# Two residual convolution blocks on one core: the low gate of the second half moves from ScalarE to VectorE

## What is computed

```
def _L0_conv_ref(x, w1, ..., w2, ..., lambdas):
    xr = tile(x, (1, 4, 1, 1))
    out = conv3x3(sign(xr), sign(w1), groups=4)
    out = relu(batchnorm(out, bn1))
    out = conv3x3(sign(out), sign(w2), groups=4)
    out = batchnorm(out, bn2) * repeat(lambdas, 64)
    out = out.reshape(B, 4, 64, H, W).sum(axis=1)
    return relu(out + x)

def _L1_conv_ref(x, masks, conv_w, in_gamma, in_beta):
    m = resize(masks, 28 x 28)
    mid = x * m
    atten = sigmoid(conv7x7([mean_c(mid), max_c(mid), m]))
    out = mid * atten
    rn = instance_norm(out) * in_gamma + in_beta
    return relu(5 * rn)

x = x + _L0_conv_ref(group_norm(x), ...)
x = x + _L1_conv_ref(group_norm(x), ...)
```

## Time and profile before

| what | value |
|---|---|
| median of 3 runs | 228.22 us (227.88 to 228.31) |
| the profiled execution, whole | 227.68 us |
| its span from first to last instruction | 225.9 us |
| granted TensorE clock, mean | 0.980 of full speed |
| TensorE busy (PE) | 198.2 us, 88% |
| ScalarE busy (ACT) | 173.8 us, 77% |
| GpSimd busy (POOL) | 154.3 us, 68% |
| VectorE busy (DVE) | 152.0 us, 67% |

### The profile page before, as it was taken

The page is one execution under the profiler, slowest core; times in us unless marked ns, Lnnn a source line. Parts: engine busy times, 40 slices in busy tenths (PEclk is TensorE's granted clock), DMA queues, the critical chain, the costliest instruction groups (busy, mean ns, idle before and its releaser), DMA issues.

```text
span 225.9 us, 8997 instructions
## 1 busy us (share of the span) xinstructions
PE 198.2 (88%) x3807; PEld 123.7 (55%) x3807; DVE 152.0 (67%) x440; ACT 173.8 (77%) x230; POOL 154.3 (68%) x216
## 2 busy tenths in 40 slices
PE   8998997999899989889998998899999998698810
PEld 3456554465566566546564665466556655366710
DVE  2676365965846887677686854775657565988874
ACT  2785889888769878798899878989899888341392
POOL 8532273727142996799769978797879877947960
PEclk9999999999999999999999999999999999999965
DMA  6998004642217040744073404431453236124117
GB/s 199 334 299 303 15 4 112 198 141 68 81 61 231 3 145 7 228 131 145 3 207 86 147 1 151 141 97 52 121 173 73 75 97 193 64 84 144 74 71 284
DMA packets 12429, 28.48 MB, mean 126 GB/s; under 512 B 2293, under 2 KB 4213, under 8 KB 12389
## 3 DMA queue, kind: packets, MB, share of 16 engines
q1 hardware_dynamic: 11653, 26.84, 38.5%
q10 hardware_dynamic: 736, 1.06, 1.5%
HBM read 21.29 MB, written 6.61 MB: 124 GB/s over the span
## 4 chain that ended last, share of the span: by engine, by line
PE 41%; POOL 19%; ACT 12%; DVE 11%; issue 9%; DMA 4%; SPq 1%; ACTq 1%; POOLq 0%; DVEq 0%
PE c L1025 10%; PE c L1004 10%; PE small L1082 6%; POOL X L437 6%; PE small L1070 5%; POOL o L432 3%; ACT S L599 3%; DMA att_b<-attention_rows 3%; ACT acc L622 3%; DVE RD L799 2%; POOL o L419 2%; DVE bnst L740 2%; ACT word L584 2%; PE y L1045 2%; DMA o<-in_w 2%
## 5 line engine op out<-in xcount | busy, mean ns | idle before, releaser
L1025 PE MATMUL c<-S,w2t 64*32 64x392 f16 x2304 | 55.1, 331 | 7.9 <-DVE RD L799 7.3
L1004 PE MATMUL c<-E,w1t 64*128 64x420 f16 (+1 forms) x576 | 54.5, 330 | 0.9 <-ACT E L578 0.7
L799 DVE SCALAR_TENSOR_TENSOR RD<-RD,c 128x784 f16<-128x784 f16 x32 | 30.8, 964 | 29.5 <-ACT RD L606 29.4
L1025 PEld LDWEIGHTS c<-S,w2t 64*32 64x32 f16 x2304 | 31.8, 92 | 26.9 <-issue 14.0
L1004 PEld LDWEIGHTS c<-E,w1t 64*128 64x128 f16 x576 | 25.5, 94 | 25.2 <-issue 7.7
L740 DVE BATCH_NORM_STATS2 bnst<-X 128x6 f32<-128x392 f32 x64 | 32.6, 552 | 6.1 <-POOL X L437 3.3
L584 ACT ACTIVATE word<-c 128x840 int32<-128x840 f32 (+1 forms) x32 | 26.0, 812 | 9.3 <-PE c L1004 9.3
L419 POOL TENSOR_TENSOR o<-o,mask_b 128x784 f32<-128x784 f32 x14 | 26.1, 1868 | 9.2 <-ACT o L628 9.2
L594 ACT ACTIVATE S<-word,thr_high 128x840 f16<-128x840 int16 (+1 forms) x32 | 30.4, 951 | 0.6
L437 POOL TENSOR_TENSOR X<-X,acc 128x784 f32<-128x784 f32 x14 | 26.0, 1856 | 6.3 <-ACT acc L622 6.3
L599 ACT ACTIVATE S<-word,thr_low_act 128x840 f16<-128x840 uint16 (+1 forms) x32 | 30.0, 937 | 0.0
(11 more groups left out here) (135 smaller groups left out, 266.6 us busy)
## 6 DMA issues: line engine op xcount, KB each, us to landing
X<-in_x SPq DMA_DIRECT2D x16, 392.0 KB, 6.1
mask_b<-mask_rows SPq DMA_DIRECT2D x32, 196.0 KB, 3.5
out<-o SPq DMA_DIRECT2D x15, 392.0 KB, 3.9
att_b<-attention_rows SPq DMA_DIRECT2D x28, 196.0 KB, 4.6
o<-in_w ACTq DMA_DIRECT2D x1, 576.0 KB, 5.2
o<-in_masks SPq DMA_DIRECT2D x1, 512.0 KB, 8.9
band<-in_band SPq DMA_DIRECT2D x1, 441.0 KB, 10.1
cs<-in_cst SPq DMA_DIRECT2D x1, 434.0 KB, 6.2
```

The costliest lines, as they stand in the source:

```text
L799: dve.scalar_tensor_tensor(RD[:, hh, 1, :], RD[:, hh, 0, :], -IMG / TINY, second_sums(t, hh), ALU.mult, ALU.add).then_inc(low2, 1)
L1004: mm = pe.matmul(c1[:, 512 - n * (1 - i):512 + n * i], w1t[64 * i:64 * i + 64, s, :], window(START[i][hh], ROWS[hh], s, E[64 * i:64 * i + ...
L1025: mm = pe.matmul(second_bank(t, hh)[at:at + Q32, LOW + HALF * i:LOW + HALF * (i + 1)], w2t[64 * r:64 * r + 64, s, q, :], window(RH * half_ ...
```

## The change

The low gate of the second half (hh = 1) is made by VectorE, with a comparison instead of a steep sigmoid: 1 where the low 16 bits of the word are above `thr_low`, else 0. It has a semaphore of its own, `gated_low1`. ScalarE keeps the high gates of both halves and the low gate of the first.

```
--- before.py
+++ after.py
             def words1(t, hh):
                 if has(t):
                     act.wait_ge(conv1_done, 2 * t + hh + 1)
+                    if hh:
+                        wait(act, gated_low1, t)
                     act.activation(word1_of(hh), first_sums(hh), ACT.Copy, bias=WORD / 2,
                                    scale=WORD / IMG).then_inc(worded1, 1)
...
-            def low_gates(t, hh):
-                if has(t):
-                    act.activation(gate_rows(t, hh, 1), by_rows(low_of(word1_of(hh))), ACT.Sigmoid,
+            def low_gates(t):
+                if has(t):
+                    act.activation(gate_rows(t, 0, 1), by_rows(low_of(word1_of(0))), ACT.Sigmoid,
                                    bias=thr_low_act[:, :], scale=LOW_STEEP).then_inc(gated_low, 1)
...
+            def late_low_gates(t):
+                if has(t):
+                    if t == 0:
+                        dve.wait_ge(cleared, CLEARED)
+                    dve.wait_ge(worded1, 2 * t + 2)
+                    wait(dve, conv2_done, 2 * t - 2)
+                    dve.tensor_scalar(gate_rows(t, 1, 1), by_rows(low_of(word1_of(1))), thr_low[:, :], None, ALU.is_gt)\
+                       .then_inc(gated_low1, 1)
...
             terms1(1)
+            late_low_gates(0)
             stats_x(2)
...
                 reduce_chunks(k - 3, 1)
+                late_low_gates(k)
                 terms2(k - 2)
                 reduce_chunks(k - 3, 2)
...
-                pe.wait_ge(gated_low, 2 * t + 1 + hh)
+                pe.wait_ge(gated_low, t + 1)
+                if hh:
+                    pe.wait_ge(gated_low1, t + 1)
```

More of the change, by code:

```diff
@@ L257, in build @@
         signed = sem("signed")
-        conv1_done, worded1, gated_low, gated_high = (
-            sem(n) for n in ("conv1_done", "worded1", "gated_low", "gated_high"))
+        conv1_done, worded1, gated_low, gated_low1, gated_high = (
+            sem(n) for n in ("conv1_done", "worded1", "gated_low", "gated_low1", "gated_high"))
         conv2_done, low2, high2 = sem("conv2_done"), sem("low2"), sem("high2")
@@ L664, in _ @@
             high_gates(0, 0)
-            low_gates(0, 0)
+            low_gates(0)
             words1(0, 1)
             high_gates(0, 1)
-            low_gates(0, 1)
             sign_x(1)
@@ L710, in _ @@
                 high_gates(k, 0)
-                low_gates(k, 0)
+                low_gates(k)
                 sign_x(k + 1)
@@ L717, in _ @@
                 high_gates(k, 1)
-                low_gates(k, 1)
                 high_sums(k, 0)
```

## The result

The changed kernel takes **251.14 us** (median of four, 249.61 to 252.7) against 228.26 of the kernel before on the same chip: a ratio of 1.101, 95% interval 1.096 to 1.106. The forecast was 233.4, its range 228.0 to 237.0: right that it is slower, wrong by 17.7 us in size. The profiled execution took 251.91 with a span of 250.1; TensorE is busy for 84% of it (88% before) and its mean granted clock is 0.932 (0.980).

What follows compares the result with a forecast made beforehand. Bound taken: a pair closed by the attention map's transfer, the loop through attention and GpSimd 0.32 shorter. A pair grows 0.54 + 1.01 - 0.32 = 1.23, five 6.15, start -0.9: 232.9, plus 0.54 for the median: 233.4 us, range 228.0 to 237.0.

Steps and rivals of the forecast that it cites:

- What bounds the pair: Even plus odd tile, 22.85 us: closed by the attention map's transfer, with a loop through attention and GpSimd only 0.32 shorter.
- A: Start of GpSimd's multiplication by the returned attention map (L432) at an odd tile's end; one A to the next, 22.85 us.
- The gate is shut out by GpSimd's operation in progress: Odd tile: VectorE's gate waits for GpSimd's last sum to end, so the power comes 1.01 us later.
- The gate's length: VectorE's new gate goes two elements at a time and takes 0.51 us; even tile's attention 0.54 later.
- The tie: Even tile: gate and GpSimd's last sum both start at 107.68; VectorE taken to win, the sum giving way by up to 0.43.
- that rival: Even tile: GpSimd wins the tie, terms 2.38 later, a pair costs 3.07, total 242.7 us; chance 0.14.
- ScalarE's relief at nothing in the pairs: Removing ScalarE's 16 low gates of 0.888 us gains nothing in steady pairs, since no step of the second loop waits for them.
- The start: Tiles 0 and 1: first convolution 0.48 earlier and a 0.41 wait before the second convolution gone, together -0.9 us.

Runs made afterwards that it cites:

- e2_onestream: Changed kernel with VectorE's gate also keeping a running maximum, so that it goes one element at a time; 237.43 us (1.034).
- e5_tie: Changed kernel with one small GpSimd copy between the attention product and the last sum of an even pass; 234.39 us (1.025).
- e1_clock: Changed kernel with 18 short TensorE products of zeros between the second mix of an even pass and the attention; 244.67 us (1.070).
- e8_dummy: Kernel before, all gates kept on ScalarE, plus the same VectorE operation written to a spare tile from pass 1 on; 252.63 us (1.104).
- e4_relief: Changed kernel, but from tile 2 on nobody makes the low gates of the second half; 227.78 us (0.9962).
- e6_odd: Changed kernel with VectorE's gate only in odd passes from tile 2 on, ScalarE making the even ones; 229.70 us (1.0049).
- e7_even: Changed kernel with VectorE's gate only in even passes from tile 2 on, ScalarE making the odd ones; 244.65 us (1.069).
- e3_late: Changed kernel with the same two-at-a-time gate moved behind the terms and third reduction on VectorE, ahead of the low sums; 228.82 us (1.0023).

## Why the prediction was wrong, step by step

- **What bounds the pair**: right for what a delay on VectorE adds: each lateness at the attention and at the power came out in the pair. (That the legs add up to a pair is no evidence, since they are read from the same rows.) Wrong for the first leg, from A to the attention: that leg is not work which A starts. In the kernel before the attention stands 8.6 behind a second convolution that waited for the low sums (0.64 at 122.67 in the earlier trace rows), and these wait for ScalarE, whose low gate was in the way:

```profile
119.92 0.89 ACT L599 ACTIVATE S<-word,thr_low_act 128x728 f16<-128x728 uint16 x1
...
120.71 0.80 ACT L606 ACTIVATE RD<-c 128x784 f16<-128x784 f32 x1
...
121.55 0.97 DVE L799 SCALAR_TENSOR_TENSOR RD<-RD,c 128x784 f16<-128x784 f16 x1 [0.96 <-ACT RD L606]
...
131.31 1.91 PE L1082 MATMUL small<-band,red 112*28 112x112 f32 x18 [0.36 <-DVE red L820]
```

  From attention to attention (108.43 to 131.31) this third loop takes 22.88, as long as the pair, and it runs through the operation that was removed.
- **The gate is shut out by GpSimd's operation in progress**: right (e2_onestream against the changed kernel). The odd power was 0.85 late, forecast 1.01.
- **The gate's length**: 0.56 to 0.61 unhindered, forecast 0.51 from the slope of operations at other forms; the 0.44 named beside it was further off. With it the even pass pays 0.63 where VectorE is first (e5_tie), forecast 0.54.
- **The tie**: this is the step that failed. I gave it to VectorE, because in the earlier trace rows a waiting VectorE went ahead of the next GpSimd operation, and priced the other outcome at 2.38 in the even pass and 242.7 in all, with a chance of 0.14. There VectorE had been waiting for half a microsecond; here both come at once, and every even pass went to GpSimd. The measured lateness is 2.28. My condition for VectorE to win, that it is queued as the multiplication ahead of the sum ends, did not decide: by the rows the gate was ready at 113.19 and that multiplication ended at 113.24. The earlier trace rows already had the tie to the hundredth; the bias row (105.55, shown above), which was not among those I had shown, tells that it is built in, and it is the same to 0.02 in every pair. A tie that cannot be settled from the rows should have had a chance near one half and a place in the range.
- **A term that was missing: TensorE's clock.** This failed too, as a term put at nothing. The sum moved the attention by 2.38 in that rival and left its length alone. A wait in front of it that grew from 0.36 to 3.13 brought the clock down; 1.6 in four pairs and 2.7 in the first, 9.1 in all (e1_clock). The rival's 242.7 plus 9.1 would have been 251.8, against 251.14 measured; that this is so close is in part luck, since its pairs were 1.0 too dear (15.4 against 14.4) and its start gained 0.5 too much.
- **ScalarE's relief at nothing in the pairs**: right in the changed kernel (e8_dummy, 0.01), wrong as it was argued. I said that the attention is not ready earlier when TensorE is; but its terms wait for a turn on TensorE, as the 0.91 at 107.57 in the earlier trace rows had shown, and where no gate stands in front it is 0.32 to 0.51 earlier after A (e4_relief, e6_odd). By itself the removal is worth 2.0 in the five pairs (e4_relief).
- **The start**: the first A came 0.39 earlier (74.03 against 74.42), forecast 0.9. The first convolution of tile 1 did start 0.71 earlier, at 17.33, but the next one at 24.92 against 24.93; in between the second convolution stands still for 0.51 with no release that the trace shows. First A's of the other kernels without zeros in front lie between 73.58 and 74.81, so I leave this term open.

## What to carry to other kernels

Before an operation moves to VectorE, look at what GpSimd runs at that very moment, and at what stands behind the new operation in VectorE's queue: the same gate cost 23 us in front of a reduction that TensorE waits for, and behind it nothing that could be told from the kernel before. Where two engines are released by one event and their legs are equally long, price both orders; a copy of 0.19 us decided 17 us here. And a wait of TensorE is priced with the work that follows it, since that may run at the lower clock.

## What was not expected of the hardware

- A tie between a VectorE gate that goes two at a time and a GpSimd two-tensor operation went to GpSimd in all five even passes of the changed kernel, and with 0.13 us of lead VectorE won (e5_tie). The row of the one shut out begins when it was ready and contains its wait (2.25 for 0.59 of work), so the two starts, 0.01 apart, do not tell who went first; the row of usual length does. Why GpSimd wins such a tie is not shown.
- The granted clock fell behind all five waits in front of the attention in the changed kernel (2.73 to 3.13), behind four of five in e7_even (2.16 to 2.75; the one of 2.41 was spared) and one of five in the profiled run of e2_onestream (1.46 to 1.87); with products of zeros in the wait it did not fall in the loop (e1_clock). The length of the wait alone does not tell: ahead of a turn behind the last A it fell at waits of 1.56 (e4_relief) and 1.65 (e6_odd) and did not at 1.65 (the changed kernel) and 1.99 (e3_late). One drop cost an attention and the convolution after it 1.6 in four of the pairs and 2.7 in the first (e1_clock against the changed kernel).
